# Causal mask of the attention's row maxima: from TensorE's extra matmuls to VectorE's max instruction

## What is computed

```python
Q = _apply_rope(split_heads(x @ Wq.T)); K = _apply_rope(split_heads(x @ Wk.T)); V = split_heads(x @ Wv.T)
logits = einsum('bhnd,bhmd->bhnm', Q, K) * scale
logits = where(causal, logits, -inf)      # query n sees keys m <= n
probs = softmax(logits, axis=-1)          # exp(logit - row maximum) / sum
attn = einsum('bhnm,bhmd->bhnd', probs, V)
```

## The kernel before

| pieces | query tile | keys | heads in a piece | mask |
|---|---|---|---|---|
| 0 | 0 | 128 | 4 | yes |
| 1, 2 | 1 | 256 | 2 | yes |
| 3-6 | 2 | 384 | 1 | yes |
| 7-10 | 3 | 512 | 1 | yes |
| 11-14 | 4 | 512 | 1 | no |
| 15 | 4 | 128 (second chunk) | 4 | yes |
| 16-19 | 5 | 512 | 1 | no |
| 20, 21 | 5 | 256 (second chunk) | 2 | yes |
| 22-25 | 6 | 512 | 1 | no |
| 26-29 | 6 | 384 (second chunk) | 1 | yes |
| 30-33 | 7 | 512 | 1 | no |
| 34-37 | 7 | 512 (second chunk) | 1 | yes |

## Time and profile before

### The profile page before, as it was taken

How to read it: one execution, slowest core, us unless ns; L and a number is a source line. 1 busy time by engine, 2 the same in 40 slices (tenths; PEclk the granted TensorE clock), 3 DMA queues, 4 the chain that set the end, 5 groups by cost and what they waited for, 6 DMA issues and landing times. The chain is left out here.

```text
span 968.8 us, 19079 instructions
## 1 busy us (share of the span) xinstructions
PE 947.7 (98%) x6068; PEld 528.1 (55%) x6068; DVE 739.5 (76%) x1835; ACT 464.1 (48%) x648; POOL 357.7 (37%) x475
## 2 busy tenths in 40 slices
PE   9999999999999999999999899999999999999996
PEld 5556333334334333433433246666665799947996
DVE  5889899999999899999996566666666466576564
ACT  2543366666766676667665722221212223364321
POOL 8995242222222222212222324333434233433434
PEclk9999799999999999999999999999999999999999
DMA  8797444446665464855621187433316232223321
GB/s 308 192 251 205 67 64 56 61 62 89 94 100 72 59 99 56 121 75 75 143 32 13 13 266 206 121 88 89 88 43 222 74 90 80 70 55 80 96 68 45
DMA packets 174815, 98.97 MB, mean 102 GB/s; under 512 B 132480, under 2 KB 161408, under 8 KB 171520
## 3 DMA queue, kind: packets, MB, share of 16 engines
q1 hardware_dynamic: 161344, 71.85, 38.7%
q10 hardware_dynamic: 8576, 12.58, 3.9%
q0 software_dynamic: 4800, 13.38, 3.7%
HBM read 65.05 MB, written 32.31 MB: 100 GB/s over the span
## 5 line engine op out<-in xcount | busy, mean ns | idle before, releaser
L1085 ACT ACTIVATE probs<-scores_ps 128x1024 f32<-128x1024 f32 (+3 forms) x384 | 289.8, 807 | 119.1 <-PE scores_ps L1026 116.3
L302 DVE TENSOR_REDUCE maxima<-max_ps 128x1 f32<-128x512 f32 (+2 forms) x352 | 228.0, 682 | 26.2 <-PE max_ps L260 19.5
L260 PE MATMUL max_ps<-k_stack,q_stack 96*128 96x512 bf16 (+3 forms) x768 | 223.8, 333 | 2.5 <-DVE maxima L297 0.5
L1164 POOL TENSOR_SCALAR_AFFINE_SELECT probs<-probs 128x512 f32<-128x512 f32 x128 | 81.3, 635 | 305.9 <-ACT probs L1085 305.1
L1026 PE MATMUL scores_ps<-q_stack,k_stack 99*128 99x512 bf16 (+3 forms) x768 | 183.5, 328 | 2.4 <-ACT probs L1085 1.0
L1046 PE MATMUL out_ps<-probs,v_ones 128*32 128x512 f32 (+3 forms) x1536 | 163.7, 498 | 2.8 <-POOL probs L1164 2.3
L260 PEld LDWEIGHTS max_ps<-k_stack,q_stack 96*128 96x128 bf16 x768 | 74.3, 97 | 156.3 <-DVE maxima L302 58.4
L297 DVE CUSTOM_DVE_ANT_0 masked_out<-max_ps,mask_wide 128x384 bf16<-128x384 f32 (+1 forms) x256 | 149.4, 621 | 9.3 <-PE max_ps L260 5.1
L1552 ACT ACTIVATE silu<-gate_ps 128x512 f32<-128x512 f32 x68 | 40.6, 597 | 211.7 <-PE gate_ps L1453 111.6
L1026 PEld LDWEIGHTS scores_ps<-q_stack,k_stack 99*128 99x128 bf16 x768 | 67.2, 98 | 65.1 <-ACT probs L1085 15.0
L1914 POOL DMA_INDIRECT out<-out_t,target_i x36 | 45.5, 1264 | 88.4 <-DVE out_t L1844 88.4
(11 more groups left out here) (210 smaller groups left out, 1247.0 us busy)
## 6 DMA issues: line engine op xcount, KB each, us to landing
k_stack<-k_parts SPq DMA_DIRECT2D x96, 128.0 KB, 4.4
q_stack<-q_parts SPq DMA_DIRECT2D x96, 128.0 KB, 7.1
q_parts<-parts SPq DMA_DIRECT2D x32, 192.0 KB, 3.2
k_parts<-parts SPq DMA_DIRECT2D x32, 192.0 KB, 3.2
sums_in<-expert_sums SPq DMA_DIRECT2D x31, 136.0 KB, 2.1
heads_rows<-heads_out SPq DMA_DIRECT2D x128, 32.0 KB, 1.9
res<-in_x SPq DMA_DIRECT2D x8, 512.0 KB, 4.6
heads_in<-heads_rows SPq DMA_DIRECT2D x64, 64.0 KB, 3.0
```

What stands on the lines that cost most here:

```text
L260: last = nc.tensor.matmul(part, self.q_stack[:ROWS, u.slot, h0 + k, t * P:(t + 1) * P], self.k_stack[:ROWS, u.slot, h0 + k, chunk * BLOCK: ...
L302: nc.vector.tensor_reduce(self.maxima[:, u.slot, chunk, h0:h0 + heads, t], self.bank("piece", u.i, n)[:, :heads * keys].rearrange("p (h k) ...
L1085: nc.scalar.activation(probs[:, s % RING, 2 * pair:2 * pair + 2, n0:], scores_ps[:, pair, :, n0:], ACT.Exp).then_inc(exp_done, 1)
L1164: nc.gpsimd.affine_select(out=tile, in_=tile, compare_op=ALU.is_ge, fill=0.0, base=0, pattern=[[0, GROUP], [1, P]], channel_multiplier=-1) ...
```

## The change

All pieces that cross the diagonal are now masked by VectorE, those of two and four heads too. For these VectorE issues one max instruction for each head over that head's columns of the bank, each with its accumulator read, in place of one reduction for the piece. TensorE's mask matmuls are gone, and with them the bfloat16 mask and identity and the three GpSimd instructions that made them, and TensorE's wait for these.

```diff
@@ find_max
             for k in range(heads):
                 part = self.bank("piece", u.i, n)[:, k * keys:(k + 1) * keys]
-                diagonal = chunk == t // BT and heads > 1
                 last = nc.tensor.matmul(part, self.q_stack[:ROWS, u.slot, h0 + k, t * P:(t + 1) * P],
                                         self.k_stack[:ROWS, u.slot, h0 + k, chunk * BLOCK:chunk * BLOCK + keys],
-                                        start=True, stop=not diagonal)
-                if diagonal:
-                    last = nc.tensor.matmul(part[:, keys - P:], self.ident_bf[:], self.mask[:],
-                                            start=False, stop=True)
+                                        start=True, stop=True)
             last.then_inc(self.piece_done, 1)
@@ reduce
-            if chunk == t // BT and heads == 1:
+            if chunk == t // BT:
                 wait(dve, self.piece_reduced, self.PIECES * u.i + n - 3)
                 stand(dve, self.dve_stood)
-                nc.vector.tensor_tensor_reduce(
-                    self.masked_out[:, n % 6, :keys], self.bank("piece", u.i, n)[:, :keys],
-                    self.mask_wide[:, BLOCK - keys:], 1.0, NEG, ALU.add, ALU.max,
-                    self.maxima[:, u.slot, chunk, h0:h0 + 1, t]).then_inc(self.piece_reduced, 1)
+                for k in range(heads):
+                    at = slice(k * keys, (k + 1) * keys)
+                    last = nc.vector.tensor_tensor_reduce(
+                        self.masked_out[:, n % 6, at], self.bank("piece", u.i, n)[:, at],
+                        self.mask_wide[:, BLOCK - keys:], 1.0, NEG, ALU.add, ALU.max,
+                        self.maxima[:, u.slot, chunk, h0 + k:h0 + k + 1, t])
+                last.then_inc(self.piece_reduced, 1)
                 continue
@@ make_masks
-        nc.gpsimd.memset(self.mask[:], 0.0).then_inc(self.consts_half, 1)
-        nc.gpsimd.tensor_copy(self.ident_bf[:], self.ident[:]).then_inc(self.consts_made, 1)
+        nc.gpsimd.memset(self.mask_wide[:], 0.0).then_inc(self.consts_half, 1)
         pool.wait_ge(self.consts_half, 1)
-        nc.gpsimd.affine_select(out=self.mask[:], in_=self.mask[:], compare_op=ALU.is_ge, fill=NEG, base=0,
-                                pattern=[[-1, P]], channel_multiplier=1).then_inc(self.consts_made, 1)
-        nc.gpsimd.memset(self.mask_wide[:], 0.0).then_inc(self.consts_half, 1)
-        pool.wait_ge(self.consts_half, 2)
@@ project, TensorE
-            pe.wait_ge(m.consts_made, 2)
             pe.wait_ge(ident_made, 1)
```

More of the change, by code:

```diff
@@ L196, in __init__ @@
         self.neg_parts = early.sb("neg_parts", [GROUP * SEQ_TILES, PARTS, P], BF16)
-        self.ident_bf = early.sb("ident_bf", [P, P], BF16)
-        self.mask = early.sb("mask", [P, P], BF16)
         self.mask_wide = early.sb("mask_wide", [P, BLOCK])
@@ L202, in __init__ @@
         self.neg_loaded = b.sem("neg_loaded")
-        self.consts_half, self.consts_made = b.sem("consts_half"), b.sem("consts_made")
+        self.consts_half = b.sem("consts_half")
         self.k_ones, self.wide_made = b.sem("k_ones"), b.sem("wide_made")
```

## The result

The changed kernel takes 974.24 us (median of 8 runs, 973.12 to 974.61), the kernel before took 969.23 in the same comparison (8 runs, 967.8 to 971.52): ratio 1.0045, 95% interval 1.0036 to 1.0055. It is slower, by an amount that lies across the bound of 0.5% which the prediction set for "can be told". The forecast was 970.8. The time is within the range (962 to 982), and a little above the forecast case's own range (967 to 974). The forecast was for 0.65 us more, the medians show 5.0 more.

The account below looks back on a forecast made before the run. The prediction took a relay of TensorE and VectorE, handing over PSUM banks, as the bound. +0.03 us a unit over 15 units (+0.45) and +0.2 at the loop's start gave 0.65 on 970.1: 970.8 us, range 962 to 982.

Parts of the forecast that it names:

- pieces 3 and 30: Two of a unit's 38 maxima pieces (0 to 37), where TensorE starts within 0.06 us of VectorE's release.
- step 1: First value product, behind piece 15: 0.23 us less on TensorE, of which 0.19 arrives because GpSimd's masking stays put.
- rival C: Short custom instructions do not overlap their tails: 10 x 0.08 = 0.8 us a unit, 983 us; chance 0.22.
- the relay: Unit's time carried by TensorE from piece 3 to 18, VectorE to 30, TensorE to about 34, VectorE to next 3.
- step 4: Behind piece 3: TensorE's 0.09 us wait for ScalarE's exponentials is absorbed, leaving +0.01 to +0.04 us a unit.
- Stretch 18 to 30: VectorE carries: starts 0.19 us earlier, pieces 20 and 21 take 0.16 to 0.19 more, piece 30 unmoved within 0.03.
- Stretch 30 to 3: VectorE carries from about piece 34: pieces 0 and 1 take longer, so piece 3 comes 0.10 to 0.13 us later.
- The start of the loop: VectorE alone carries in front, then TensorE at 1.2 GHz: between -0.5 and +0.8 us, taken as +0.2.
- case A: Forecast case, the relay closes even: 970.8 us, from 967 to 974; chance 0.56.
- B: Rival that TensorE alone is the bound: 15 x 0.93 = 14 us go, 956 us; chance 0.16.
- D: Rival of a clock drop inside the loop as TensorE waits longer: 2.7 us a stretch, two 976 us; chance 0.06.

Follow-up runs that it names:

- pair_0_1: Kernel before, with only pieces 0 and 1 of the multi-head pieces masked by VectorE, TensorE keeping masks 2, 15, 20, 21: 970.81 us, ratio 1.0014.
- pair_2_15: Kernel before, with only pieces 2 and 15 of the multi-head pieces masked by VectorE, TensorE keeping masks 0, 1, 20, 21: 969.47 us, ratio 1.0007.
- mid_after: Changed kernel with VectorE's combining of maxima moved between pieces 1 and 2, and the turn, negation and split later: 971.51 us, ratio 1.0021 against the kernel before.
- mid_hybrid: As mid_after, but TensorE keeps the masks of pieces 20 and 21: 969.97 us, ratio 1.0002 against the kernel before.
- no_mask: Kernel before with the mask left out in pieces of two and four heads, plain reductions kept: 963.42 us, ratio 0.994.
- mid kernels: Three kernels with the combining of maxima moved between pieces 1 and 2, under the old, changed or mixed masks: 970.59, 971.51 and 969.97 us.
- both_masks: Changed kernel with TensorE's mask matmuls also kept, so pieces of two and four heads are masked twice: 977.31 us, ratio 1.0086 against the kernel before.
- norm_after: Changed kernel with VectorE's scaling of a unit's first outputs moved to before piece 16 of the next unit: 1008.38 us, ratio 1.0397 against the kernel before.

## Why the prediction came out as it did

**The bound was read rightly.** That VectorE sets the starts of pieces 3 and 30, and TensorE most of what lies between 3 and 18, is shown three ways: equal work in pair_0_1 and pair_2_15 differs by 0.19 a unit by its place; taking all these masks away gives 0.44 and not 0.93; adding TensorE's back costs 0.17 and not 0.93. Between 3 and 18 TensorE is not alone: the first value product there waits for GpSimd (step 1 below).

**The prices were right.** A head with 128 keys costs 0.21, one with 256 keys 0.34 (0.34 and 0.21 were taken). So rival C fell: no tail shows between two custom instructions at any width. The estimate by the Trainium skill (VectorE: DVE Perf Modes, section on the TRN2 errata), 0.26 and 0.39, is not borne out as a price in a row: 0.21 to 0.61 for 128 to 512 keys is a straight line with a fixed part of 0.08. It is near the printed lengths of single instructions, 0.28 and 0.42, which here overlap the next one.

**The steps along the relay,** against the table (the prediction's value first):
1. Stretch 3 to 18: 0.28 shorter, measured 0.21. The first value product came 0.10 forward instead of 0.19 (pair_2_15, where piece 15 alone lost its masks in this stretch: 11.05 against 11.15). GpSimd's masking, ahead of it on its own engine, in the kernel after:

```profile
309.03 0.64 POOL L1155 TENSOR_SCALAR_AFFINE_SELECT probs<-probs 128x512 f32<-128x512 f32 x1 [8.17 <-ACT probs L1076]
```

and TensorE, the piece before it and the product:

```profile
309.30 0.38 PE L257 MATMUL max_ps<-k_stack,q_stack 96*128 96x512 bf16 x1
309.81 0.64 PE L1037 MATMUL out_ps<-probs,v_ones 128*32 128x512 f32 x4
```

The masking ends at 309.67 and the product starts 0.14 later; I had put it 0.05 behind the masking's end. The rest of the 0.21 is the absorbed wait for ScalarE (step 4), 0.11 where 0.09 was put (pair_0_1: 11.04).
2. Stretch 18 to 30: 0.16 to 0.19 longer, measured 0.19. Right, and mid_after against mid_hybrid gives the same alone (0.20).
3. Stretch 30 to 3: 0.10 to 0.13 longer, measured 0.20. Pieces 0 and 1 with their last read take 1.62 (298.19 to 299.81), as summed to 0.02. But from the combining instruction to piece 0 it is 0.26 (297.93 to 298.19). In the timeline of the kernel before it was 0.19, to 296.57:

```profile
296.38 0.27 DVE L312 TENSOR_TENSOR maxima<-maxima 128x16 f32<-128x16 f32 x1
```

 For a masked piece's later start (two waits and a marker in front of a custom instruction) I took 0.03; it is 0.07.

So the step that failed is the closing of the sum: +0.03 a unit was the difference of three terms of 0.1 to 0.3, and errors of 0.07 and 0.08 with the same sign made it +0.18. The two mis-sized terms are the first value product (0.19 forward, measured 0.10) and the stretch to piece 3 (0.10 to 0.13, measured 0.20). Over 15 units the 0.18 are 2.7 us, 2.3 more than was put; the loop's 3.0 is slightly more, as single units grew by more than the others, the tenth and eleventh (28.26 and 28.32) above all. The start of the loop came 0.3 later instead of 0.2. Of the 5.0 us between the medians that leaves 1.7 without a cause: 0.6 behind the loop, and 1.1 by which the medians lie further apart than the profiled executions. There was some luck too: the forecast was built on 970.1, the median of three executions, while eight gave 969.23, which brought it 0.9 nearer to the result; and the measured 0.45% lies just inside the bound of 0.5%, which its interval crosses. The mechanism of case A stands; its size was off, and its own range (to 974) allowed for errors in the price of the custom instruction alone, not for the handing over between engines, where they were.

**Rivals.** B fell by no_mask. C fell by the prices. D did not come: between 113 and 521 us the granted clock was 1.00 in both kernels.

**What should have shown it.** "0.2 to 0.5 us each" of wait at pieces 3 and 30 was right for 3 (0.30); at 30 the trace of the kernel after prints no wait, and the two starts there (318.19 and, from the pair's end, 318.53) are 0.34 apart. The prices of the pieces, 0.85 and 0.69 where 0.84 and 0.68 were put, were right. "27.93 to 28.0" between the combining instructions was wrong (28.13). No row of the trace before shows a masked piece right behind the combining instruction. But it does show that a masked piece starts later behind what it waits for than a plain one (0.22 against 0.04 us behind TensorE, in the last section), and the 0.03 was taken without a look at such a row.

Open: the 0.6 us behind the loop, the longer first units of the mid kernels and of both_masks, and the first combining instruction of pair_2_15, which came 0.7 later than before.

## What to carry to other kernels

Where two engines hand buffers to each other, find for each stretch of the loop which of them starts right after the other's release, and count a change only there: the same work (one four-head and one two-head piece) moved cost 0.08 a unit at one place and gave 0.11 at the other. When the expected effect is the small difference of several terms, give it the sum of their errors as its range, and look for work on the carrying engine that can go where the other carries, which here took the changed kernel from 974 to 967 us, where moving the masks alone had cost 5. Before a store is made to wait, see what stands behind it in its queue.

## What the runs showed of the hardware

- The custom maximum with a mask costs 0.21, 0.34, 0.48 and 0.61 us for 128, 256, 384 and 512 keys when it stands in a row, with the accumulator's read beside the next one; alone at the end of a piece the read adds 0.08.
- An instruction that waits for TensorE starts later when it is masked: in the kernel before, a 512-key one started at 302.15, 0.22 us after the modelled end of its matmul (301.54 + 0.39), and a plain reduction at 307.89 only 0.04 after its own (307.46 + 0.39). The masked one has two waits and a marker ahead; whether these or the kind of instruction cost it was not tried.
- TensorE started the value product 0.14 us behind GpSimd's end in the kernel after, and matmuls 0.05 to 0.07 behind VectorE's end at pieces 3, 4 and 30.
- In norm_after TensorE's matmuls waited four times for loads between 250 and 400 us, 8.7 us in all and 3.1 at most, and the granted clock was 0.93 on average there, against 1.00 in the kernel before; with 0.30 us of waiting at piece 3 of each unit it was 0.991 over the whole span of the kernel after, as in the kernel before.
- SyncE issued its DMAs in the order of the program: one store that waited for a later VectorE instruction held the loads behind it back, by 9 us in the unit shown, and the kernel took 1008 us; with the store behind those loads it took 967.
